# Group statistics moved to ScalarE, M kept in its PSUM bank, and one change of order on GpSimd in a preactivated linear-attention kernel

## The reference

```
g   = group norm of x: 32 groups of 8 channels, mean and variance over 8 x 6400 values, eps 1e-5
xt  = g as 6400 tokens x 256 channels
q, k, v = split(xt @ qkv_w.T + qkv_b)          # 256 each
q   = relu(q);  k = relu(k + pos_enc)
per head (8 heads of 32 channels):
  z  = 1 / (q . sum over tokens of k + 1e-6)
  kv = sum over tokens of k (outer) v
  out = (q @ kv) * z
y   = x + out @ proj_w.T + proj_b
```

## Time and profile before

| | |
|---|---|
| median of 3 runs | 2663.91 us (2662.24 to 2664.78) |
| profiled execution | 2665.23 us, span 2663.4 us |
| PE busy | 2593.6 us (97%) |
| DVE busy | 1603.5 us (60%) |
| ACT busy | 1661.0 us (62%) |
| POOL busy | 1974.8 us (74%) |
| mean granted TensorE clock | 0.998 of full |

### The profile page before, as it was taken

The page is one execution under the profiler, slowest core; times in us unless marked ns, Lnnn a source line. Parts: engine busy times, 40 slices in busy tenths (PEclk is TensorE's granted clock), DMA queues, the critical chain, the costliest instruction groups (busy, mean ns, idle before and its releaser), DMA issues.

```text
span 2663.4 us, 44657 instructions
## 1 busy us (share of the span) xinstructions
PE 2593.6 (97%) x15812; PEld 2214.4 (83%) x15812; DVE 1603.5 (60%) x2500; ACT 1661.0 (62%) x2544; POOL 1974.8 (74%) x1218
## 2 busy tenths in 40 slices
PE   4989999999999999999999999999999999999998
PEld 4878888788888888888888888888878888788886
DVE  6655656566665565656656555566666666555547
ACT  4656666566666656656566666656656566665664
POOL 5958777687786868768687786877768678686875
PEclk9999999999999999999999999999999999999999
DMA  7557867677776767767677677776868777675668
GB/s 257 185 171 240 274 219 260 221 258 248 240 262 230 267 221 256 265 225 251 229 251 263 229 262 250 253 256 217 263 217 267 237 249 257 211 256 192 229 208 296
DMA packets 323163, 641.99 MB, mean 241 GB/s; under 512 B 24704, under 2 KB 46080, under 8 KB 322944
## 3 DMA queue, kind: packets, MB, share of 16 engines
q1 hardware_dynamic: 322944, 639.14, 71.5%
HBM read 519.25 MB, written 119.80 MB: 240 GB/s over the span
## 4 chain that ended last, share of the span: by engine, by line
PE 80%; DVE 6%; issue 5%; ACT 4%; POOL 3%; DMA 2%; ACTq 0%; SPq 0%; DVEq 0%; POOLq 0%
PE banks L582 18%; PE banks L606 17%; PE banks L639 16%; PE banks L594 12%; PE banks L596 6%; PE banks L573 5%; PE banks L624 4%; ACT xn L1051 2%; DVE kk L875 1%; DVE stats L853 1%; DVE banks L870 1%; POOL hl L1253 1%; ACT kk L1073 1%; POOL kacc L1267 1%; ACT xt L1068 1%
## 5 line engine op out<-in xcount | busy, mean ns | idle before, releaser
L1267 POOL TENSOR_TENSOR kacc<-kacc,kt 128x512 f32<-128x512 f32 x368 | 477.4, 1297 | 330.8 <-ACT kt L1080 328.6
L582 PE MATMUL banks<-wqk,hl 128*128 128x256 f32 x4608 | 646.4, 290 | 12.8 <-POOL hl L1253 12.8
L1253 POOL TENSOR_TENSOR hl<-xn,hl 128x512 fp32r<-128x512 f32 x384 | 493.9, 1309 | 213.1 <-ACT hl L1063 212.9
L859 DVE TENSOR_TENSOR xt<-banks,xt 128x512 fp32r<-128x512 f32 x400 | 274.5, 686 | 567.6 <-ACT xt L1068 567.5
L606 PE MATMUL banks<-hl,wqk 128*128 128x512 f32 x2304 | 601.2, 396 | 12.9 <-DVE xr L889 12.9
L582 PEld LDWEIGHTS banks<-wqk,hl 128*128 128x128 f32 x4608 | 576.0, 191 | 17.7 <-POOL hl L1253 17.7
L594 PE MATMUL banks<-kk,xt 128*128 128x512 f32 x1600 | 584.5, 399 | 4.1 <-DVE kk L875 4.1
L639 PE MATMUL banks<-uhl,mhl 128*128 128x512 f32 (+1 forms) x2316 | 542.4, 383 | 2.1 <-DVE xr L889 2.1
L639 PEld LDWEIGHTS banks<-uhl,mhl 128*128 128x128 f32 x2316 | 424.2, 188 | 89.8 <-issue 2.5
L606 PEld LDWEIGHTS banks<-hl,wqk 128*128 128x128 f32 x2304 | 406.0, 188 | 108.1 <-DVE xr L889 17.1
L1287 POOL TENSOR_TENSOR q<-q,zb 128x1024 f32<-128x1024 f32 x180 | 433.7, 2409 | 78.0 <-DMA zb<-z_rows 77.8
(11 more groups left out here) (117 smaller groups left out, 2406.8 us busy)
## 6 DMA issues: line engine op xcount, KB each, us to landing
posb<-pos_plus_bk SPq DMA_DIRECT2D x375, 256.0 KB, 4.9
xs<-in_x SPq DMA_DIRECT2D x184, 512.0 KB, 6.8
xa<-in_x SPq DMA_DIRECT2D x184, 512.0 KB, 6.1
xr<-in_x SPq DMA_DIRECT2D x184, 512.0 KB, 3.9
zb<-z_rows SPq DMA_DIRECT2D x184, 512.0 KB, 6.0
y<-xr SPq DMA_DIRECT2D x184, 512.0 KB, 7.1
z_rows<-zt SPq DMA_DIRECT2D x32, 256.0 KB, 5.4
xr<-in_pos SPq DMA_DIRECT2D x25, 256.0 KB, 5.1
```

The costliest lines, as they stand in the source:

```text
L582: last = mm(psK[:, par(n, h), i * C:(i + 1) * C], hl_of(t)[:, a, c, s:s + P], wqk[:, w, c, C:2 * C], start=(j == 0), stop=(j == len(terms) ...
L1253: g.tensor_tensor(hl_of(t)[:, 1, :, s], xn_of(n, t)[:, :, s], hl_of(t)[:, 0, :, s], ALU.subtract).then_inc(xl_ready, 1)
L1267: g.tensor_tensor(both, both, kt[:, par(n, h), :], ALU.add).then_inc(ks_done, 1)
```

## The change

Of the small statistics DVE keeps the negated mean, the deviation, the two values got from the group variance (variance + eps, and -0.5 times that), and the reciprocal of the root, which moves ahead of the residual in step 11. ScalarE takes the rest, one activation per channel block with a [128, 1] scale pointer (and bias pointer): deviation squared plus variance (gn_square), and grs x (-0.5 var), x grs + 1.5, x grs, and mean x rstd (gn_rstd). In batches 1 and later gn_square stands in step 10 and gn_rstd in step 11, both between u's high part and key_high of the odd half. In batch 0 gn_square(1) and gn_rstd(1) stand at the ends of steps 10 and 11, and for batch 0's own statistics both stand ahead of the weight copies. M's total stays in psX bank 1, and its high and low part are taken from there, in all batches but the last. POOL makes xn_low(n + 1, 0) ahead of key_sum(n, 24).

```diff
             def gn_offsets(n):
                 dve.wait_ge(gn_mean, n + 1)
-                dve.wait_ge(gn_step, 10 * n + 1)
-                v.tensor_copy(gmean[:], psX[:, 1, 0:CC])
+                dve.wait_ge(gn_step, 4 * n + 1)
+                v.tensor_scalar(gmean[:], psX[:, 1, 0:CC], -1.0, None, ALU.mult)
                 v.tensor_tensor(gdev[:], mv[:, :, 0], psX[:, 1, 0:CC], ALU.subtract).then_inc(gn_step, 1)
-                v.tensor_tensor(gtmp[:], gdev[:], gdev[:], ALU.mult).then_inc(gn_step, 1)
-                v.tensor_tensor(gvar[:], gtmp[:], mv[:, :, 1], ALU.add).then_inc(gn_step, 1)
...
             def gn_variance(n):
                 dve.wait_ge(gn_var, n + 1)
-                v.tensor_scalar(gvar[:], psX[:, 1, 0:CC], GN_EPS, None, ALU.add).then_inc(gn_step, 1)
+                v.tensor_scalar(gvar[:], psX[:, 1, 0:CC], GN_EPS, None, ALU.add)
+                v.tensor_scalar(gdev[:], psX[:, 1, 0:CC], GN_EPS, -0.5, ALU.add, ALU.mult).then_inc(gn_step, 1)
-            def gn_rstd(n):
+            def gn_inverse(n):
                 dve.wait_ge(gn_sqrt, n + 1)
                 v.reciprocal(grs[:], gtmp[:]).then_inc(gn_step, 1)
-                v.tensor_tensor(gdev[:], grs[:], grs[:], ALU.mult).then_inc(gn_step, 1)
-                v.tensor_tensor(gdev[:], gdev[:], gvar[:], ALU.mult).then_inc(gn_step, 1)
-                v.tensor_scalar(gdev[:], gdev[:], -0.5, 1.5, ALU.mult, ALU.add).then_inc(gn_step, 1)
-                v.tensor_tensor(rstd[:], grs[:], gdev[:], ALU.mult).then_inc(gn_step, 1)
-                v.scalar_tensor_tensor(out=nbias[:], in0=gmean[:], scalar=-1.0, in1=rstd[:],
-                                       op0=ALU.mult, op1=ALU.mult).then_inc(gn_ready, 1)
...
+            def gn_square(n):
+                act.wait_ge(gn_step, 4 * n + 2)
+                for c in range(CC):
+                    last = a(gvar[:, c:c + 1], gdev[:, c:c + 1], ACT.Identity, bias=mv[:, c, 1:2], scale=gdev[:, c:c + 1])
+                last.then_inc(gn_spread, 1)
...
+            def gn_rstd(n):
+                def each(out, src, scale, bias, done):
+                    for c in range(CC):
+                        k = slice(c, c + 1)
+                        if bias is None:
+                            last = a(out[:, k], src[:, k], ACT.Identity, scale=scale[:, k])
+                        else:
+                            last = a(out[:, k], src[:, k], ACT.Identity, bias=bias, scale=scale[:, k])
+                    last.then_inc(done, 1)
+                act.wait_ge(gn_step, 4 * n + 4)
+                each(gtmp, grs, gdev, None, gn_newton)
+                act.wait_ge(gn_newton, 3 * n + 1)
+                each(gvar, gtmp, grs, halves3, gn_newton)
+                act.wait_ge(gn_newton, 3 * n + 2)
+                wait(act, xn_ready, NBLK * n)
+                each(rstd, gvar, grs, None, gn_newton)
+                act.wait_ge(gn_newton, 3 * n + 3)
+                each(nbias, gmean, rstd, None, gn_ready)
...
# ScalarE, first_step (batch 0)
                     save_q(*q_at(0, t), 1, 0)
                 if t == 10:
+                    gn_square(1)
                     gn_root(1)
+                if t == 11:
+                    gn_rstd(1)
# ScalarE, step (batches 1 and later)
                 if has_u(n, t):
                     u_step(n, t)
+                if t == 10 and n + 1 < B:
+                    gn_square(n + 1)
+                if t == 11 and n + 1 < B:
+                    gn_rstd(n + 1)
                 if t < LAST:
                     key_high(n, 2 * t + 1)
# ScalarE, start
+            gn_square(0)
             gn_root(0)
+            gn_rstd(0)
             act.wait_ge(w_loaded, 16 * 5)
# TensorE
-                pe.wait_ge(gn_step, 10 * n + 4)
+                pe.wait_ge(gn_spread, n + 1)
                 mm(psX[:, 1, 0:CC], gavg[:], gvar[:], start=True, stop=True).then_inc(gn_var, 1)
...
                     elif ot == 0:
-                        pe.wait_ge(m_sum, on + 1)
+                        pe.wait_ge(ml_ready, on + 1)
# DVE, step 2 (and m_low likewise)
-                    m_total(n - 1, psX[:, 1])
+                    m_total(n - 1, psX[:, 1], in_bank(psX[:, 1]))
# ScalarE
-                wait(act, ml_ready, n)
+                wait(act, kv_done, n)
                 a(mt[:], psG[:, :, C:2 * C], ACT.Copy).then_inc(gl_copied, 1)
# POOL, step
+                if t == LAST and n + 1 < B:
+                    xn_low(n + 1, 0)
                 key_sum(n, 2 * t)
...
                 if t < LAST:
                     xn_low(n, t + 1)
-                elif n + 1 < B:
-                    xn_low(n + 1, 0)
```

More of the change, by code:

```diff
@@ L76, in build @@
         hmask = sb("hmask", [P, HPC])
-        consts = sb("consts", [P, 2])
-        ones, zeps = consts[:, 0:1], consts[:, 1:2]
+        consts = sb("consts", [P, 3])
+        ones, zeps, halves3 = consts[:, 0:1], consts[:, 1:2], consts[:, 2:3]
         biases = sb("biases", [P, 3, CC])
@@ L127, in build @@
         gn_var = sem("gn_var")
+        gn_spread = sem("gn_spread")
         gn_sqrt = sem("gn_sqrt")
+        gn_newton = sem("gn_newton")
         gn_ready = sem("gn_ready")
@@ L190, in build, with in_bank @@
         z_places = [xn[:, 0], xn[:, 1], kt[:], zb[:, 0], zb[:, 1]]
+        def in_bank(bank):
+            return bank.rearrange("p (c n) -> p c n", c=CC)
         def size(t):
@@ L697, in bank_free @@
                         elif ot == 7 and on + 2 < B:
-                            pe.wait_ge(gn_step, 10 * (on + 2) + 2)
+                            pe.wait_ge(gn_step, 4 * (on + 2) + 2)
                         elif ot == 8 and on + 2 < B:
-                            pe.wait_ge(gn_step, 10 * (on + 2) + 5)
+                            pe.wait_ge(gn_step, 4 * (on + 2) + 3)
                 output(on, ot, u, psX[:, 0:2], bank_free)
@@ L910, in kv_masked, with m_total, m_low @@
                 last.then_inc(kvm_ready, 1)
-            def m_total(n, bank):
+            def m_total(n, bank, total):
                 dve.wait_ge(m_done, n + 1)
                 for c in range(CC):
-                    last = v.scalar_tensor_tensor(out=mt[:, c, :], in0=bpb[:, c, :], scalar=ksc[:, c:c + 1],
+                    last = v.scalar_tensor_tensor(out=total[:, c, :], in0=bpb[:, c, :], scalar=ksc[:, c:c + 1],
                                                   in1=bank[:, c * C:(c + 1) * C], op0=ALU.mult, op1=ALU.add)
                 last.then_inc(m_sum, 1)
-            def m_low(n):
+            def m_low(n, total):
                 dve.wait_ge(mh_ready, n + 1)
                 mw = mhl_last if n == B - 1 else mhl
-                v.tensor_tensor(mw[:, 1, :, :], mt[:], mw[:, 0, :, :], ALU.subtract).then_inc(ml_ready, 1)
+                v.tensor_tensor(mw[:, 1, :, :], total, mw[:, 0, :, :], ALU.subtract).then_inc(ml_ready, 1)
             def invert(n, g, parts=(0, 1)):
@@ L943, in step @@
                     g_total(n - 1)
+                if t == 11 and n + 1 < B:
+                    gn_inverse(n + 1)
                 if has_out(n, t) and (n, t) != (B - 1, LAST):
@@ L954, in step @@
                     if t == 2 and junction:
-                        m_low(n - 1)
+                        m_low(n - 1, in_bank(psX[:, 1]))
                     key_low(n, 2 * t + 1)
@@ L963, in step @@
                         gn_variance(n + 1)
-                    if t == 11:
-                        gn_rstd(n + 1)
                 if first(n):
@@ L998, in finish @@
                 residual(n - 2, LAST - 2, psX[:, 0:2])
-                m_total(n - 1, psT)
+                m_total(n - 1, psT, mt)
                 invert(n - 1, 1, (1,))
-                m_low(n - 1)
+                m_low(n - 1, mt[:])
                 residual(n - 2, LAST - 1, psX[:, 0:2])
@@ L1012, in _ @@
             v.memset(zeps, Z_EPS)
+            v.memset(halves3, 1.5)
             v.memset(kvm[:], 0.0)
@@ L1026, in _ @@
             gn_variance(0)
-            gn_rstd(0)
+            gn_inverse(0)
             for n in range(B):
@@ L1115, in z_plus, with m_high @@
                 a(zt[:, g, :], bank, ACT.Identity, bias=zeps).then_inc(zt_ready, 1)
-            def m_high(n):
+            def m_high(n, total):
                 act.wait_ge(m_sum, n + 1)
                 wait(act, o_done, CC * NBLK * n)
-                a(mhl[:, 0, :, :], mt[:], ACT.Copy).then_inc(mh_ready, 1)
+                a(mhl[:, 0, :, :], total, ACT.Copy).then_inc(mh_ready, 1)
             def m_high_last():
@@ L1167, in step @@
                 if t == 2 and not first(n):
-                    m_high(n - 1)
+                    m_high(n - 1, in_bank(psX[:, 1]))
                 if t < LAST:
```

14 lines of the change are left out of this document (3 added, 11 removed).

## The result

The changed kernel takes 2638.81 us in the median of 4 runs (2638.19 to 2639.41), the kernel before 2663.07 beside it (2657.16 to 2664.78). The ratio is 0.9913, 95% interval 0.9896 to 0.9930: faster by 24.3 us. The direction and the places were right; of the gain in the profiled execution (26.2 us) a third was missing from the sum.

The account below looks back on a forecast made before the run. TensorE, busy 2593.6 of 2663.4 us, was taken to bound the kernel; -21.4 + 3.5 + 0.3 + 3.3 - 3.3 = -17.6 us gave 2646.3 us from 2663.91, range 2641 to 2658.

Parts of the forecast that it names:

- the stalled end: Batch end where POOL's multiply delays nbias on DVE and the query product waits; ten of 14, 2.14 us each, 21.4 gained.
- the second table load: At the start, in front of Sqrt: could show, costing 0.4 us in the variance product's shadow if it lasts 1.28.
- The lowered clock behind batch 0: Granted clock averaging 0.62 over 4.5 us after batch 0's idle stretch; its loss of 1.5 us was to go.
- step 1: Rstd chain on ScalarE, batches 1 and later: holds it 2.33 us, stall about 0.25 in 14 ends, +3.5 us.
- D: Rival: no stall at all, chain under 2.1 us, and a start at +2.7; 2642 us, 15% chance.
- the first part: What bounds the kernel now: TensorE's idle time at batch ends, each stalled end priced at 2.14 us against a free one.
- free end: Batch end where normalisation and query product start without idle time; 161.19 us between mean products against 163.33 with a stalled end.
- Part 2: POOL's low part of x ahead of the last key sum: the key product's 0.55 us wait goes, inside the 2.14.
- B: Rival: ScalarE's chain turns the change round, decided at a chain of 3.6 us; 2670.9 us at the upper bound, 8% chance.
- A: Rival: longer activations, all eight of the chain at 0.40 us, 11.8 in place of 3.5; 2654.6 us, 15% chance.
- C: Rival: something else holds the ends (row of z for POOL's multiply, the residual's input); about 2664 us, 7% chance.
- my text: On DVE beside POOL: the reciprocal reads one tensor and can't be caught; only 128x2 instructions reading two SBUF tensors exceed 0.2 us.

Follow-up runs that it names:

- the order alone: The kernel before with one edit: at step 12 POOL makes the low part of the next x ahead of the last key sum; 2651.65 us.
- the order undone: The changed kernel with POOL's old order at step 12 put back; 2653.16 us.
- POOL yielding: The kernel before with one wait added: at step 12 of batches 1 to 14 POOL starts its multiply only when nbias is ready; 2645.59 us.
- the start repaired: The changed kernel with gn_rstd(0) moved behind ScalarE's two weight copies; 2635.8 us.
- the doubled chain: The changed kernel with eight more 128x1 activations, into a spare tile, in ScalarE's rstd chain; 2660.86 us.
- both repairs: The changed kernel with gn_rstd(0) behind the weight copies and batch 0's squares and chain ahead of key_high of the odd half; 2634.74 us.

## Why the prediction was wrong in size

What was right, and is shown, is first the reading of the stalled end: DVE instructions caught by POOL's multiply hold up the normalisation, and the key product is held by POOL's order besides (the order alone, the order undone and POOL yielding separate the two). The first transposes start at 33.36 (said 33.4), paid because of ScalarE's order (the start repaired). That this number was hit is in part luck: the second table load is there and keeps the root 0.4 back, where next to nothing was booked for it, and the chain behind the reciprocal takes 2.1 us (26.02 to 28.16) where 2.5 were booked. The wait for the squares in batch 0 is 1.57 (said 1.6). The lowered clock behind batch 0 is gone. The window of the changed kernel (engines' busy times, granted clock, DMA share, GB/s):

```profile
157.00:161.50 4.50, 3.81 (x27) 3.27 (x26) 2.14 (x5) 2.79 (x6) 3.77 (x3) 1.00 0.74 240
```

Wrong were two terms of the sum.

The first is in step 1: "a dependent pair starts 0.09 after the one before it", from which came 2.33 us, a stall of 0.24 in 14 ends and +3.5. The 0.09 was read between the normalisation and a 128x1024 activation. Behind the short ones it is 0.03: in the timeline above the first pair ends at 626.92 and the next starts at 626.95. The single activations take 0.286 and 0.379 us, where 0.30 and 0.40 were priced. With 0.06 less three times and pairs of 0.47 to 0.48 and 0.67 where I put 0.51 and 0.71, 1.99 us come out. The point where waits begin was put too early as well, at 2.09 instead of the 2.25 that follows from the doubled chain. A chain 0.1 to 0.25 us from the point where it starts to cost was multiplied by 14, and no stall at all stood only in a rival (D, 15%).

The second is in the first part: the free end as the measure of an undisturbed batch. It "gave 161.19", so a stalled end was worth 2.14. But a free end had its own wait for POOL. In the free end of batch 3 before, the timeline has POOL's low part and TensorE thus:

```profile
642.07 2.53 POOL L1253 TENSOR_TENSOR hl<-xn,hl 128x512 fp32r<-128x512 f32 x2
642.82 0.60 PE L573 MATMUL banks<-ident,xn 128*128 128x128 f32 x4
...
643.41 1.69 PE L582 MATMUL banks<-wqk,hl 128*128 128x256 f32 x12
```

The first half is ready at 642.07 + 1.3 = 643.4, and the key product starts with it, 0.59 after the transposes started. It is 0.58 or 0.59 in all four free ends. Undisturbed, at an inner step, it starts 0.35 after them:

```profile
629.35 0.60 PE L573 MATMUL banks<-ident,xn 128*128 128x128 f32 x4
...
629.70 1.67 PE L582 MATMUL banks<-wqk,hl 128*128 128x256 f32 x12
```

The view of waits does not list the loss, because the modelled ends of the transposes reach to the key product's start. The order alone shows it by itself: free batches are 160.93 us apart there. That makes 0.26 us in 14 ends, 3.6 us, all of which the new order removes. Part 2 had worked out that POOL's low part would be in time, and booked nothing for the free ends.

3.5 + 3.6 is most of the 8.7 us by which profile and sum differ. 0.6 more is in the end of batch 0, and 1.1 lie in places that the change does not touch: a key product 0.8 us late for POOL in batch 11 of before, and the tail. In the tail chance has a share: behind the same wait of 2.1 us the granted clock was 0.66 in the profile of before and 1.00 in that of the change, but 0.66 again when the change was profiled once more.

Of the rivals, B is a question of length, and its point of 3.6 us is about right: at 3.48 the doubled chain leaves 2.6 us of the gain. A did not come, with 0.286 and 0.379; it would have cost some 6 us, an estimate (eight at 0.40 with waits of 0.03 are 2.7, 14 x 0.45). C has fallen, as the ends became free in each kernel that took away the late nbias; where the row of z came late in the kernel before, the end was a free one. D has the right place, no stall, but books too little for the order.

The Trainium skill ("ScalarE: Activation LUTs", rules for kernel authors) says to use VectorE and not ScalarE for add and mul. These runs do not speak against it: with POOL's new order and POOL yielding, DVE's chain (2635.8 us) does as well as ScalarE's with both repairs (2634.74).

## What to carry to other kernels

Where two engines' instructions collide, ask first which of them can be put off for nothing: one wait on POOL was worth 17.8 us here (2663.43 to 2645.59), moving the victims to another engine without the new order 10.3, net of what the change costs at the start and in batch 0. A stretch without listed idle time is no proof of full speed; set the start-to-start distances of the same matmuls in several places side by side before calling one undisturbed. And when small work is moved to an engine that runs in order, look at its first and single occurrences: the change paid 3.3 us at the start and a wait of 1.6 in batch 0, and better places gave back 2.4 and 2.1.

## What the runs showed of the hardware

- A DVE instruction with a single small SBUF input is caught too, against my text: L840 (tensor_scalar, 128x2) of the kernel before beside POOL's key sum, in the free end of batch 3. The reciprocal L834 took 0.15 to 0.17 us throughout, and in the batches, all 15 times, a POOL instruction was in flight beside it. The Trainium skill ("SBUF — State Buffer", who interferes with whom) has tensor_scalar among the operations that can take the port pair shared with GpSimd; the trace agrees.

```profile
634.37 1.28 POOL L1267 TENSOR_TENSOR kacc<-kacc,kt 128x512 f32<-128x512 f32 x1 [0.16 <-ACT kt L1080]
...
634.46 1.23 DVE L840 TENSOR_SCALAR gdev<-gdev 128x2 f32<-128x2 f32 x1
```

- The second table load is there, and takes 1.28 us. The timeline of the start in the changed kernel:

```profile
23.64 0.67 ACT L1034 ACTIVATE gvar<-gdev,mv 128x1 f32<-128x1 f32 x2 [21.63 <-DVE gdev L829]
24.33 1.28 ACT L1039 ACT_TABLE_LOAD   x1
...
25.62 0.20 ACT L1039 ACTIVATE gtmp<-gvar 128x2 f32<-128x2 f32 x1
```

  It starts 0.02 after the squares, and the root follows 0.01 behind it, 0.4 later than its operand. The Trainium skill ("ScalarE: Activation LUTs", what a table load costs) gives 2.66 us with a drain; the drain's part is not seen here.

- The granted clock after about the same idle time (2.10 and 2.08 us, in front of the first output products of the tail) was 0.66 over five us in the kernel before, a mean of the levels of 1.2 and 2.4 GHz, and 1.00 in the changed one, the upper level throughout. It is not the change: its second profile has 0.66 over 2593 to 2598 us, again behind 2.08 us of idle time. What decides it stays open.

```profile
2618.00:2623.00 5.00, 4.86 (x20) 4.36 (x21) 4.22 (x6) 3.17 (x4) 5.00 (x3) 0.66 0.79 254
```

```profile
2592.00:2597.00 5.00, 4.43 (x24) 3.79 (x25) 4.87 (x7) 3.83 (x5) 5.00 (x3) 1.00 0.61 168
```

- The kernel before spread over 18 us from run to run (2654.49 to 2672.95), the changed one over 3.4 (2637.36 to 2640.77). In the kernel before each stalled end costs 2.4 us, and which ends are stalled hangs on when the row of z arrives and differs between traces (with the order alone again ten, but others). That their number makes the spread is likely and not shown, as only one execution of the kernel before has a trace.
